# C of a unit computed once as 16 rows and spread over 32 channels by DMA through device memory, in place of four products and four copies

## The reference

```
u  = silu(conv3(x))                                  # 3 taps along the tokens
BC = u @ W_bc + b_bc ;  B, C = split(BC)             # 16 states each, per token
A  = -exp(A_log)                                     # (128, 16)
dt = softplus((u @ W_dt + b_dt) @ W_dtp + b_dtp)     # (tokens, 128)
h[t, d, n] = exp(A[d, n] * dt[t, d]) * h[t-1, d, n] + B[t, n] * x[t, d] * dt[t, d]
y[t, d]    = sum over n of C[t, n] * h[t, d, n]  +  x[t, d] * Dcoeff[d]
x1 = layernorm(x + y)
q(.) = blockwise FP4 quantise and dequantise (blocks of 16)
out = layernorm(x1 + q(silu(q(x1) @ q(w_gate).T) * (q(x1) @ q(w_up).T)) @ q(w_down).T)
```

## Time and profile before

| | |
|---|---|
| median of 3 runs | 338.46 us (337.42 to 338.52) |
| span of the profiled execution | 335.0 us; the median of the runs is 3.46 us above it |
| busy in the span: DVE, POOL, PE, ACT | 299.6, 264.3, 262.6, 250.8 us |
| spacing of units in the middle | about 34.8 us |
| DMA: bytes moved, of which `dt_rep` on SP's queue | 21.85 MB; 124 DMAs of 128 KB |

### The profile page before, as it was taken

How to read it: one execution, slowest core, us unless ns; L and a number is a source line. 1 busy time by engine, 2 the same in 40 slices (tenths; PEclk the granted TensorE clock), 3 DMA queues, 4 the chain that set the end, 5 groups by cost and what they waited for, 6 DMA issues and landing times.

```text
span 335.0 us, 4031 instructions
## 1 busy us (share of the span) xinstructions
PE 262.6 (78%) x1172; PEld 129.6 (39%) x1172; DVE 299.6 (89%) x329; ACT 250.8 (75%) x547; POOL 264.3 (79%) x138
## 2 busy tenths in 40 slices
PE   2666976768877897989697969797986779688892
PEld 1222422223322343633353336243542345355592
DVE  3869998999999999999999999999998999986920
ACT  2477889748975788798979887989788577535746
POOL 0075675688459998999999999999999989965840
PEclk9979899799957997999999999999898999999998
DMA  3690662810192009220742055104701000100012
GB/s 44 151 216 8 142 144 63 188 31 0 33 198 53 3 0 201 51 63 0 156 98 64 0 127 126 31 0 97 157 1 31 2 0 0 34 0 0 1 33 63
DMA packets 19261, 21.85 MB, mean 65 GB/s; under 512 B 6112, under 2 KB 15144, under 8 KB 19240
## 3 DMA queue, kind: packets, MB, share of 16 engines
q1 hardware_dynamic: 18520, 21.05, 27.7%
q10 hardware_dynamic: 720, 0.56, 0.9%
HBM read 2.72 MB, written 2.10 MB: 14 GB/s over the span
## 4 chain that ended last, share of the span: by engine, by line
POOL 56%; issue 13%; DVE 11%; ACT 7%; PE 6%; SPq 4%; DMA 2%; DVEq 0%; POOLq 0%; ACTq 0%
POOL product L895 26%; DVE db L1140 5%; POOL hq L945 5%; POOL qh_norm L935 5%; POOL qh_magic L915 5%; POOL qh_norm L910 5%; DVE states L1160 5%; SPq L509 3%; POOL qx_magic L915 2%; POOL qx_norm L910 2%; POOL qx_norm L921 2%; POOL xq L929 2%; ACT ps_decay L565 1%; ACT L555 1%; POOL qh_magic L983 1%
## 5 line engine op out<-in xcount | busy, mean ns | idle before, releaser
L895 POOL TENSOR_TENSOR product<-states,c_rep 128x1024 f32<-128x1024 f32 x59 | 139.4, 2381 | 23.2 <-DVE states L1160 20.3
L565 ACT ACTIVATE ps_decay<-dt_rep,aneg 128x512 f32<-128x512 f32 x128 | 87.0, 691 | 23.3 <-DVE states L1160 15.9
L1160 DVE TENSOR_TENSOR_SCAN states<-ps_decay,db 128x512 f32<-128x512 f32 x64 | 74.9, 1201 | 0.3
L1140 DVE SCALAR_TENSOR_TENSOR db<-ps_b,bbc_rep,dt_rep 128x2048 f32<-128x2048 f32 x31 | 72.1, 2325 | 0.4 <-PE ps_b L1484 0.4
L1160 DVE TENSOR_TENSOR_SCAN states<-ps_decay,states,db 128x512 f32<-128x512 f32 x54 | 66.6, 1260 | 1.0 <-ACT ps_decay L565 1.0
L1484 PE MATMUL ps_b<-u_feat,wbc_rep 128*128 128x512 f32 x64 | 39.1, 695 | 4.7 <-DVE db L1140 4.3
L1478 PE MATMUL ps_prep<-u_feat,wbc_rep 128*128 128x512 f32 x56 | 35.2, 715 | 6.6 <-ACT c_rep L642 6.6
L555 ACT ACT_TABLE_LOAD x26 | 33.4, 1283 | 0.5
L1442 PE MATMUL ps_y<-product,gather 128*32 128x512 f32 x248 | 31.8, 599 | 1.0 <-POOL product L895 1.0
L642 ACT ACTIVATE c_rep<-ps_prep,bbc_rep 128x512 f32<-128x512 f32 x28 | 19.1, 683 | 10.7 <-PE ps_prep L1478 10.7
L1526 PE MATMUL ps_f<-gate_t,xq_t 128*128 128x352 f32 x48 | 17.4, 485 | 8.1 <-ACT hidden L649 6.3
(11 more groups left out here) (250 smaller groups left out, 501.1 us busy)
## 6 DMA issues: line engine op xcount, KB each, us to landing
dt_rep<-dtx SPq DMA_DIRECT2D x124, 128.0 KB, 2.4
x_tok<-in_L_attn_x SPq DMA_DIRECT2D x8, 256.0 KB, 3.0
out<-y_out SPq DMA_DIRECT2D x7, 256.0 KB, 2.3
dt_rep<-dtx ACTq DMA_DIRECT2D x4, 128.0 KB, 3.7
out<-y_out SPq DMA_DIRECT2D x2, 128.0 KB, 1.8
hidden<-in_L_ffn_w_down SPq DMA_DIRECT2D x1, 176.0 KB, 3.4
x_feat<-in_L_attn_x SPq DMA_DIRECT2D x8, 0.5 KB, 2.0
hidden<-in_L_ffn_w_gate SPq DMA_DIRECT2D x1, 128.0 KB, 2.9
```

The lines of the kernel that those rows point to most:

```text
L565: nc.scalar.activation(ps_decay[BANK_OF[i]][:], dt_rep[p][:, c, 0, :], ACT.Exp, scale=aneg[:, c, m:m + 1]).then_inc(decay_done, 1)
L895: nc.gpsimd.tensor_tensor(product[:, j % PRODUCTS], groups(s, 2 * j, 2), over(c_rep[p][:, j // SET_PAIRS, :], 2), ALU.mult).then_inc(produ ...
L1140: nc.vector.scalar_tensor_tensor(out=db[m % DB][:], in0=over(ps_b[:], QUADS), scalar=bbc_rep[:, 0, m:m + 1], in1=dt_rep[p][:, :, 1, :], op ...
L1160: nc.vector.tensor_tensor_scan(out=groups(s, k, 1)[:, 0, :], data0=ps_decay[BANK_OF[s.at(GROUPS, k)]][:], data1=db[k // QUADS % DB][:, k % ...
```

## The change

C of a unit is made by one product with the plain 16 weight columns, into rows 0 to 15 of `ps_prep`. ACT adds the bias and copies them to `c_rows` (16 x 512). SP writes `c_rows` to a scratch in device memory (32 KB), waits until it has landed, and reads it back with 16 DMAs, each of which repeats one row over 32 partitions of `c_rep` (64 KB each). The products of POOL wait for the DMAs of their set (`c_in`). The last products of DVE read `c_rep` instead of the bank. One small load (`bias_c`) is added at the start.

```diff
-    "pe x": 11, "pe conv": (13,), "pe z": 15, "pe B": (13, 1, 5, 10), "pe C": (5, 6, 8, 10),
+    "pe x": 11, "pe conv": (13,), "pe z": 15, "pe B": (13, 1, 5, 10), "pe C": 4,
...
-PREP_MM, PREP_EVAC = 3 + SETS, 1 + SETS
+PREP_MM, PREP_EVAC = 4, 2
...
+                (bias_c[:], b_bc[N:2 * N].rearrange("(p a) -> p a", a=1)),
...
+            def spill_c(a, o):
+                sp.wait_ge(prep_evac, a.at(PREP_EVAC, 2))
+                sp.dma_start(c_spill[o][:], c_rows[:]).then_inc(c_out, 16)
+
+            def replicate_c(a, o):
+
+                sp.wait_ge(c_out, a.at(16))
+                if a.beyond(2):
+                    sp.wait_ge(product_done, a.at(PAIRS, -PAIRS))
+                for m in range(SETS):
+                    for n in range(STATES):
+                        row = m * STATES + n
+                        sp.dma_start(c_rep[o][n * E:(n + 1) * E, m, :],
+                                     c_spill[o][row:row + 1, :].broadcast_to([E, UNIT])).then_inc(c_in[m], 16)
+
...
                 if a is not None:
                     replicate(a, 1 - p)
+                    spill_c(a, 1 - p)
                 if b is not None:
                     load_halo(b, p)
+                if a is not None:
+                    replicate_c(a, 1 - p)
                 if h is not None:
                     store(h, 1 - p)
...
-            def c_of(a, o, m):
-                act.wait_ge(prep_mm, a.at(PREP_MM, 4 + m))
-                if m == 0 and a.beyond(2):
-                    act.wait_ge(product_done, a.at(PAIRS, -PAIRS))
-                nc.scalar.activation(c_rep[o][:, m, :], ps_prep[:], ACT.Identity,
-                                     bias=bbc_rep[:, 1, m:m + 1]).then_inc(prep_evac, 1)
+            def c_of(a):
+                act.wait_ge(prep_mm, a.at(PREP_MM, 4))
+                if a.beyond(2):
+                    act.wait_ge(c_out, a.at(16, -16))
+                nc.scalar.activation(c_rows[:], ps_prep[0:N, :], ACT.Identity, bias=bias_c[:]).then_inc(prep_evac, 1)
...
-                elif j == 0:
-                    pool.wait_ge(prep_evac, s.at(PREP_EVAC, PREP_EVAC))
+                elif j % SET_PAIRS == 0:
+                    pool.wait_ge(c_in[j // SET_PAIRS], s.at(16 * STATES))
...
-            dve.wait_ge(vec_in, 16 * 3)
+            dve.wait_ge(vec_in, 16 * 4)
...
-                nc.vector.scalar_tensor_tensor(
-                    out=product[:, j % PRODUCTS, k % 2, :], in0=ps_prep[:], scalar=bbc_rep[:, 1, SETS - 1:SETS],
-                    in1=groups(s, k, 1)[:, 0, :],
-                    op0=ALU.add, op1=ALU.mult).then_inc(last_product, 1)
+                nc.vector.tensor_tensor(product[:, j % PRODUCTS, k % 2, :], c_rep[1][:, SETS - 1, :],
+                                        groups(s, k, 1)[:, 0, :], ALU.mult).then_inc(last_product, 1)
...
-                nc.tensor.matmul(ps_prep[:], wbc_rep[:, 1, m], u_feat[o][:], start=True, stop=True).then_inc(prep_mm, 1)
+            def c_of(a, o):
+                pe.wait_ge(dtx_done, a.at(1, 1))
+                nc.tensor.matmul(ps_prep[0:N, :], wbc[:, N:2 * N], u_feat[o][:], start=True, stop=True).then_inc(prep_mm, 1)
```

More of the change, by code:

```diff
@@ L215, in build @@
         bbc = sb("bbc", [128, 2 * N])
+        bias_c = sb("bias_c", [N, 1])
+        c_rows = sb("c_rows", [N, UNIT])
         table_in = sb("table_in", [128, 2])
@@ L226, in build @@
         center = sb("center", [128, 128])
+        c_spill = [nc.dram_tensor(f"c_spill{h}", [N, UNIT], fp32, kind="Internal").ap() for h in range(2)]
         WCOLS = 2 * 3 * D + INNER
@@ L396, in build @@
         b_mm = sem("b_mm")
+        c_in = [sem(f"c_in{m}") for m in range(SETS)]
+        c_out = sem("c_out")
         decay_done = sem("decay_done")
@@ L769, in step @@
                         down(h, 1 - p, k, ps_f2, True)
-                    if a is not None:
-                        for m, slot in enumerate(prep_places(a)["act C"]):
-                            if k == slot:
-                                c_of(a, 1 - p, m)
+                    if a is not None and k == prep_places(a)["act C"]:
+                        c_of(a)
                     if f is not None and k == AT["act x1"]:
@@ L1616, in step @@
                         down(h, k, ps_f2, (hidden_done, g.at(TILES, TILES)) if k == AT["pe hq"] else None)
[L1617 to L1620 removed]
+                    if a is not None and k == prep_places(a)["pe C"]:
+                        c_of(a, 1 - p)
                     if b is not None:
```

17 lines of the change are left out of this document (4 added, 13 removed).

## The result

The changed kernel takes 342.12 us (median of 4 runs, 340.73 to 345.07) against 338.49 us for the kernel before on the same chip (4 runs, 337.42 to 339.08). The ratio is 1.0122, with a 95% interval of 1.0073 to 1.0172: slower by 1.2%, some 4 us. The prediction was 338.6 us, "no change", with a range up to 341.1; the time lies 1.0 us above that range. Two executions later on, one of the kernel before (504.98 us) and one of e7 (1291.5 us), are far outside all others and are left out of the ratios and of this account.

What follows compares the result with a forecast made beforehand. DVE was taken as the bound in the middle units. Span 335.0 + 0.2 (column of x) - 0.2 (stretch at 98) = 335.0, plus 3.46 from span to median: 338.5, stated as 338.6 us; range 336.3 to 341.1.

Steps and rivals of the forecast that it cites:

- The bound in the middle: Middle units: DVE is full, so taking copies from ACT and products from PE was put at 0 gain, at most 2.7 us.
- The reads: SP's 16 reads of C per unit: 7.2 us (5.4 to 10), landing in 1.8 to 2.4 us, cost 0 in middle units.
- Rivals 3 and 4: Slow reads make units wait for C, 356 us (chance 0.08); the reads' fixed costs don't overlap, about 420 us (0.01).
- The rest: Start and tail: bias_c load costs 0, at most 0.3 us; DVE's last four products go from 0.75 to 0.68 us, counted 0.
- The tight place: unit 1: Column of x for unit 2's convolution issued later, behind the scratch write: 0.2 us lost, bounds 0 to 0.45.
- Rival 2: TensorE's clock falls in more windows as PE idles longer; 0.5 us a unit in five more units, 341.1 us; chance 0.17.
- The gain in the stretch at 98: Spacing from 98.16 to 133.37 us could shrink with fewer products in the way: 0.2 us gain, between 0 and 0.4.

Runs made afterwards that it cites:

- e7: Changed kernel, last products reading PSUM again, first step with column of x before the scratch write and six unread matmuls before unit 2's convolution: 338.69 us.
- e11: The changed kernel run once more, unaltered, for a second profile and more times: 341.79 us, ratio 1.0116 against the kernel before.
- e5: Changed kernel, last products reading C from PSUM again and, in the first step, column of x issued before the scratch write: 340.13 us, ratio 1.0054.
- e8: Kernel before plus only the scratch write and 16 repeated reads, 32 KB each, into a buffer nothing reads: 338.63 us, ratio 1.001.
- e3: Changed kernel plus three unread PE products a unit where C's products were, last products as in the change: 345.45 us, ratio 1.0229.
- e2: Kernel before with only the changed last DVE products, which read C from SBUF instead of the bank: 341.3 us, ratio 1.0067.

## Why the prediction was wrong

**Right.** The bound in the middle: with three copies of four gone from ACT, the units keep their 34.8 us, and relief on ACT and PE is worth nothing there. The reads: 16 in 7.28 us in a middle unit (7.2 estimated) and 8.78 in unit 1; landing 2.0 us. POOL never waits for `c_rep`, dt is not late, and POOL's pair of products beside the reads of unit 1 (45.42) keeps its 4.66 us. Rivals 3 and 4 are refuted by the same rows. The write of the scratch landed in 1.9 us. The 3.46 us between span and median, which the sum adds, was read as something outside the span; some 1.1 us of it is that the profiled execution was a fast one. Both parts went into the sum together, so its base of 338.5 was right all the same.

**Wrong, first step: "The rest", the last four products of DVE.** The text costed them from 0.75 to 0.68 us each, a small gain set to 0. They took 1.2 to 2.7 us and cost the tail 1.8 or 5.0 us. The 0.68 us came from a row of `dtx<-ps_prep,x_feat`, whose first input lies in PSUM; DVE's instructions with two large inputs in SBUF in the kernel before (at 6.4, 7.1, 8.8, 12.4, 15.8 and 307.03 us) ran while POOL had nothing under way, so no row there shows such a meeting. The row was taken by form and size, and what mattered was where its inputs lie. The sentence "beside POOL, whose chain is the later one" named the neighbour and didn't ask whether the two can run together. The rule of the Trainium skill that is quoted above says that they can't; the prediction did not use it.

**Wrong, second step: "The tight place: unit 1".** The lateness of the column was sized well (0.65 us later on PE in the profile, 0.17 in e11, 0.45 forecast; e5 gets 0.2 to 0.5 back for it). What the step left out is that the same place loses the products of C, and that the work behind them moves forward, so PE runs dry ahead of the wait: it waits 2.85 us, where the forecast had 0.9 to 1.4. The term of 0.2 us, with an upper bound of 0.45, measured 2.4 to 3.1 us at `qx_norm`, of which the convolution at 1.2 GHz makes 2.4 to 2.7 (5.25 and 5.46 us against 2.81).

**Rival 2, half right.** It named this mechanism, put it on the other side, and priced it at 341.1. But it looked for it in the windows with the up products and argued against it from the middle (a clock of 1.00 from 137 to 172), where PE stays busy. The place was the convolution of unit 2, where PE waits for a DMA with nothing queued ahead. Where it looked, the clock is lower too (0.50 from 100 to 112 in the first profile and in e11, 0.78 and 0.88 before), but DVE waits clearly longer for an up product in one unit of each profile only: 1.73 us at 122.44 in e11 and 1.06 at 192.16 in the first profile (after a clock of 0.52 from 184 to 186), in place of 0.45. It had 0.17. The advice on idle gaps that it cites from the Trainium skill stands in TensorE: Matmul & The Clock Gate under Why this matters for your kernels. The trace agrees at the convolution: 2.85 us without work, then a clock of 0.50.

**The gain in the stretch at 98** (0.2 us) is not steady: the spacing is 34.84 us in the first profile and 35.97 in e11, against 35.21 before. The sum had +0.2 and -0.2; what the typical profile (e11, span +4.8) shows is +2.4 at unit 1, +0.8 in the stretch at 98, -0.1 from there to the last `qx_norm`, and +1.8 in the tail, with 5.0 in place of 1.8 in some executions. About 1.1 us of the +4.8 is the fast profile of the kernel before: by the medians e11 is 3.7 us slower. That the stretch gained 0.4 us in the first profile is luck, not the relief that was forecast.

## What to carry to other kernels

- When an operand of a DVE instruction moves from PSUM to SBUF, price it anew, above all if its other input is in SBUF and POOL works beside it: it may wait for the end of POOL's operation. Look up the duration in a row with the same places of inputs, not only the same form.
- When products are taken from PE, go to each place where they stood and ask what PE does next and what it waits for there. Work that the profile calls idle-engine work can be what keeps TensorE at 2.4 GHz for a product on the critical chain. A few unread products right ahead of it gave back about 1.9 us here; elsewhere in PE's order they cost more than they gave.
- Before two profiles are compared, find how far apart they are ahead of the place in question, and how far each profiled execution lies from the median. Here both were about 1 us, as much as one of the effects.
- Moving a broadcast from PE and ACT to DMA cost at most 0.4% in itself (e8, with reads of half the size; e7 with the whole change); the loss lay in two side effects. With both mended the kernel is where it was, because the engines relieved were not the bound.

## What the runs showed of the hardware that was not expected

- DVE's 128x512 product with both inputs in SBUF took 0.83 to 2.75 us beside POOL, ending 0.54 or 0.55 us after one of POOL's operations wherever the ends can be compared (the first profile and e11); with one input in PSUM it took 0.75 us beside the same operations. A shift of phase of 0.8 us (a start 1.67 or 2.46 us after POOL's pair) changed the cost of the tail from 1.8 to 5.0 us, and it went with a granted clock of 1.00 or of 0.50 to 0.57 a dozen us earlier.
- A repeated read of one row of the scratch into 32 partitions (64 KB) has an issue time of 0.46 us in a middle unit (7.28 us for 16) and lands in 2.0 us, no slower than a copy from SBUF to SBUF (2.3 us for 128 KB).
- The convolution's three products (six matmul records) took 2.74 to 2.81 us at a granted clock of 1.00 and 5.1 to 5.5 us at 0.50, after 2.4 to 2.9 us without work on PE (4.41 us in e3, where the clock came back during it); with 0.9 to 1.5 us without work (the kernel before, e2, e8) and the products of C ahead of it, the clock stayed at 1.00.
